# Skip weights carried by two existing loads, 14 instead of 17 zero matmuls, and a new order of work on every engine

## The reference

```
q   = layernorm(x)                               # over the last axis, 256
kv  = einsum('bhil,bhjl->bijhl', k, k)           # k = v = ctx, all pairs of the 8 channels
y   = irfft(rfft(kv, 512) * rfft(ssm_kernel, 512))[..., :256]
out = y + kv * D                                 # D: one skip weight per head
x1  = x + einsum('bijhl,bhil->bjhl', out, q)
g   = silu(layernorm(x1) @ Wg'); u = layernorm(x1) @ Wu'
out = x1 + (g * u) @ Wd'                         # W' = (int - 128) * scale
```

## Time and profile before

| | us |
|---|---|
| median of 3 runs | 78.2 (78.01 to 78.25) |
| profiled execution, first to last instruction (span) | 76.7 |
| PE busy | 70.7 (92%) |
| DVE busy | 63.9 (83%) |
| POOL busy | 54.6 (71%) |
| ACT busy | 46.7 (61%) |
| memory traffic | 8.29 MB, nearly all before 25 us |

### The profile page before, as it was taken

How to read it: one execution, slowest core, us unless ns; L and a number is a source line. 1 busy time by engine, 2 the same in 40 slices (tenths; PEclk the granted TensorE clock), 3 DMA queues, 4 the chain that set the end, 5 groups by cost and what they waited for, 6 DMA issues and landing times.

```text
span 76.7 us, 1495 instructions
## 1 busy us (share of the span) xinstructions
PE 70.7 (92%) x469; PEld 57.8 (75%) x469; DVE 63.9 (83%) x191; ACT 46.7 (61%) x115; POOL 54.6 (71%) x73
## 2 busy tenths in 40 slices
PE   4999988879999999999999999999999999999920
PEld 3767735568798777787888797988897989899810
DVE  0088399969999999899999999999999993786760
ACT  0601483275859587976868468746767798766400
POOL 5004798799889599299899949459627899939230
PEclk9999999999999999999999999999999999999995
DMA  0498999999997000000000000000000222200404
GB/s 5 132 256 279 386 344 295 285 384 397 386 353 220 13 0 0 0 0 4 4 9 0 0 0 0 0 0 0 0 9 4 68 68 68 68 9 0 137 0 137
DMA packets 7304, 8.29 MB, mean 108 GB/s; under 512 B 992, under 2 KB 6400, under 8 KB 7296
## 3 DMA queue, kind: packets, MB, share of 16 engines
q1 hardware_dynamic: 6912, 8.00, 31.7%
q10 hardware_dynamic: 384, 0.19, 0.8%
HBM read 7.12 MB, written 1.07 MB: 107 GB/s over the span
## 4 chain that ended last, share of the span: by engine, by line
PE 58%; DMA 15%; DVE 14%; SPq 3%; ACT 3%; issue 2%; DVEq 0%; ACTq 0%
PE conv L1010 18%; PE turn L957 8%; PE down L1029 8%; DMA k_ext<-ctx_ext 8%; DMA toeplitz<-taps 7%; PE conv L977 6%; PE conv L988 6%; PE conv L986 6%; DVE hidden L733 3%; DVE terms L718 2%; PE turn L939 2%; DVE terms L721 2%; PE turn L1029 2%; SPq L310 2%; ACT gate_act L508 1%
## 5 line engine op out<-in xcount | busy, mean ns | idle before, releaser
L1010 PE MATMUL conv<-f_parts,wgu 128*128 128x256 f16 x176 | 21.6, 273 | 0.3
L1010 PEld LDWEIGHTS conv<-f_parts,wgu 128*128 128x128 f16 x176 | 16.7, 98 | 3.5 <-DVE hidden L733 0.8
L376 POOL TENSOR_TENSOR products<-k_ext 128x512 f32<-128x512 f32 (+1 forms) x16 | 18.0, 1144 | 0.6 <-DMA k_ext<-ctx_ext 0.6
L508 ACT ACTIVATE gate_act<-conv,sg_sb 128x256 f32<-128x256 f32 (+1 forms) x24 | 11.2, 471 | 4.6 <-PE conv L1010 4.0
L258 POOL TENSOR_TENSOR h_lo<-hidden,h_hi 128x256 fp32r<-128x256 f32 x18 | 12.9, 729 | 1.4 <-ACT h_hi L513 1.3
L733 DVE SCALAR_TENSOR_TENSOR hidden<-conv,su_sb,gate_act 128x256 f32<-128x256 f32 (+1 forms) x24 | 11.3, 479 | 3.1 <-ACT gate_act L508 2.7
L977 PE MATMUL conv<-products,toeplitz 128*128 128x288 f32 x32 | 11.2, 434 | 0.3 <-DVE terms L725 0.3
L365 POOL TENSOR_TENSOR rstd_f<-variance_f,minus_half 128x1 f32<-128x1 f32 x8 | 5.5, 683 | 7.9 <-DVE variance_f L694 7.9
L718 DVE TENSOR_TENSOR terms<-conv,q_ext 128x512 f32<-128x512 f32 x16 | 10.8, 678 | 0.0
L986 PE MATMUL conv<-products,toeplitz 128*128 128x288 f32 x32 | 10.8, 422 | 0.0
L988 PE MATMUL conv<-products,toeplitz 128*128 128x288 f32 x32 | 10.4, 406 | 0.0
(11 more groups left out here) (64 smaller groups left out, 119.8 us busy)
## 6 DMA issues: line engine op xcount, KB each, us to landing
k_ext<-ctx_ext SPq DMA_DIRECT2D x3, 384.0 KB, 6.1
toeplitz<-taps_pad SPq DMA_DIRECT2D x2, 512.0 KB, 7.9
out<-x_sb SPq DMA_DIRECT2D x8, 128.0 KB, 1.7
toeplitz<-taps SPq DMA_DIRECT2D x3, 256.0 KB, 5.3
wg_int<-wg_t SPq DMA_DIRECT2D x1, 704.0 KB, 8.2
wu_int<-wu_t SPq DMA_DIRECT2D x1, 704.0 KB, 9.5
wd_int<-wd_t SPq DMA_DIRECT2D x1, 640.0 KB, 8.6
x_sb<-x SPq DMA_DIRECT2D x1, 512.0 KB, 7.0
```

What stands on the lines that cost most here:

```text
L376: nc.gpsimd.tensor_tensor(view(products[:, n:n + 1], first * MADE + GROUP, [[MADE, halves], [GROUP, 4], [1, GROUP]]), view(k, 0, [[EXT * B ...
L508: nc.scalar.activation(gate_act[up_lanes(t), i % 2, t, :], gate_of(i, t), ACT.Silu, scale=sg_sb[gate_lanes(t), t:t + 1]).then_inc(gate_act ...
L1010: done = nc.tensor.matmul(bank_of(i, t)[:, n, :], wgu[:, c, column:column + P], f_parts[:, i % 2, part, c, :], start=(c == 0 and part == 0 ...
```

## The change

1. `skip_all` is no longer a load of its own. The 16 weights stand ahead of each partition's row of k in memory, and the first k transfer brings them along (208 instead of 192 numbers a partition).
2. `skip_sb` is gone too. The weights stand in column 0 of the taps array, which was padding, and POOL reads them from there. POOL now waits for one transfer and not for two.
3. DVE no longer waits for `skip_loaded`.
4. `fill` issues 14 zero matmuls and not 17.
5. The lists of calls of PE, DVE, ACT and POOL are written in a new order. What they contain is otherwise the same; SP's list is the same.

```diff
-        skip_sb = sb("skip_sb", [H, 1])
-        skip_all = sb("skip_all", [P, H])
+        k_skip = sb("k_skip", [P, H + H * HALVES * EXT * B])
+        skip_all = k_skip[:, 0:H]
+        k_ext = k_skip[:, H:].rearrange("p (h c n) -> p h c n", h=H, c=HALVES)
...
             def load_k(first, last, done):
-                sp.dma_start(k_ext[:, first:last], ctx_ext[:, first:last]).then_inc(done, 16)
+                row = HALVES * EXT * B
+                columns = slice(H + first * row if first else 0, H + last * row)
+                sp.dma_start(k_skip[:, columns], ctx_skip[:, columns]).then_inc(done, 16)
...
-                nc.gpsimd.tensor_tensor(taps_sb[:, P:P + 1], taps_sb[:, P:P + 1], skip_sb[:, :],
+                nc.gpsimd.tensor_tensor(taps_sb[:, P:P + 1], taps_sb[:, P:P + 1], taps_sb[:, 0:1],
...
-            pool.wait_ge(taps_loaded, 32)
+            pool.wait_ge(taps_loaded, 16)
...
-            act.dma_start(skip_all[:, :], skip.rearrange("h a -> (h a)").partition_broadcast(P)).then_inc(skip_loaded, 16)
             act.dma_start(x_sb[:, 0, :], x[0:P, :]).then_inc(x_loaded[0], 16)
             act.dma_start(taps_sb[:, :], taps).then_inc(taps_loaded, 16)
-            act.dma_start(skip_sb[:, :], skip).then_inc(taps_loaded, 16)
...
             all_products(0, 0, 1)
+            dve.wait_ge(x_loaded[0], 16)
+            stats_of_q(0)
             all_products(0, 1, 2)
             dve.wait_ge(anti_ready, 1)
-            dve.wait_ge(skip_loaded, 16)
...
-            fill(turn[:, 0:2 * P], 17)
+            fill(turn[:, 0:2 * P], 14)
```

More of the change, by code:

```diff
@@ L71, in up_lanes, with build @@
     return slice(0, P) if t < FULL else slice(TAIL, P)
-def build(nc, x, ctx_ext, taps, skip, wg_t, s_gate, wu_t, s_up, wd_t, s_down, taps_pad, out):
+def build(nc, x, ctx_skip, taps, wg_t, s_gate, wu_t, s_up, wd_t, s_down, taps_pad, out):
     with ExitStack() as ctx:
@@ L578, in _ @@
             gate(0, 0)
-            wrap(4)
             gate(0, 1)
             hidden_high(0, 0)
-            squares(15)
+            wrap(4)
+            norm_q(6)
             gate(0, 2)
-            norm_q(6)
+            act.wait_ge(k_loaded[5], 16)
+            squares(12)
+            evict_q(5)
+            evict_q(6)
             hidden_high(0, 1)
-            evict_q(5)
+            gate(0, 3)
             hidden_high(0, 2)
-            gate(0, 3)
+            gate(0, 4)
+            hidden_high(0, 3)
+            squares(13)
             norm_f(2)
-            evict_q(6)
-            hidden_high(0, 3)
-            gate(0, 4)
+            wrap(5)
+            norm_f(3)
+            high_f(2)
+            gate(0, 5)
+            squares(14)
             norm_q(7)
[L594 to L597, removed]
             high_f(3)
+            evict_q(7)
             hidden_high(0, 4)
-            evict_q(7)
-            wrap(6)
             hidden_high(0, 5)
             gate(1, 0)
+            norm_f(4)
+            squares(15)
             gate(1, 1)
-            hidden_high(1, 0)
-            norm_f(4)
-            hidden_high(1, 1)
+            wrap(6)
             gate(1, 2)
             high_f(4)
+            hidden_high(1, 0)
             gate(1, 3)
+            gate(1, 4)
+            hidden_high(1, 1)
             hidden_high(1, 2)
@@ L613, in _ @@
             norm_f(5)
-            gate(1, 4)
             high_f(5)
@@ L777, in _ @@
             stats_of_q(2)
+            stats_of_q(3)
             moments_of_q(2)
-            shift_of_q(1)
             multiply_terms(0)
-            stats_of_q(3)
-            variance_of_q(2)
             multiply_terms(1)
             moments_of_q(3)
+            variance_of_q(2)
+            multiply_terms(2)
+            variance_of_q(3)
             dve.wait_ge(direct_loaded[3], 16)
@@ L1089, in _ @@
             convolve(11)
+            turn_q(6, x1_ready, 4)
             gates(0, 3)
             gates(0, 4)
-            turn_q(6, x1_ready, 4)
+            sum_terms(4, q_ready, 7)
             convolve(12)
-            sum_terms(4, q_ready, 7)
+            downs(0, 0)
             gates(0, 5)
-            downs(0, 0)
             turn_f(2, x1_ready, 5)
@@ L1102, in _ @@
             gates(1, 0)
+            downs(0, 1)
+            sum_terms(5, q_ready, 8)
             gates(1, 1)
-            downs(0, 1)
+            gates(1, 2)
+            turn_f(4, x1_ready, 6)
             downs(0, 2)
-            sum_terms(5, q_ready, 8)
-            gates(1, 2)
             downs(0, 3)
-            turn_f(4, x1_ready, 6)
-            gates(1, 3)
             downs(0, 4)
             downs(0, 5)
+            gates(1, 3)
+            gates(1, 4)
             sum_terms(6, f_ready, 5)
             convolve(15)
-            gates(1, 4)
             gates(1, 5)
@@ L1137, in _ @@
             gates(3, 2)
+            downs(2, 3)
             gates(3, 3)
-            downs(2, 2)
-            downs(2, 3)
             downs(2, 4)
```

234 lines of the change are left out of this document (114 added, 120 removed).

## The result

The changed kernel takes 84.5 us (84.2 to 84.7, 4 runs) against 78.2 (78.0 to 78.3, 4 runs): 8.2% slower, ratio 1.082, 95% interval 1.079 to 1.085. Forecast were 77.2 us, with a range of 76.2 to 78.3 and a chance of 0.14 for slower. The profiled execution was timed at 84.48 us, its span is 82.6. Times are medians of all runs of a kernel; a few runs were in a slower state, and the ratios leave those out.

The account below looks back on a forecast made before the run. PE and DVE, both full from 20.1 to 30.6 us, were taken as the bound, with time winnable before. Span 76.7 + 0 (loads) + 0 (fill) - 1.0 (early order) + 0 (later) = 75.7, plus 1.5 gives 77.2 us; range 76.2 to 78.3.

Parts of the forecast that it names:

- the sum over DVE: DVE up to 25 us: same work, transfer waits 1.65 us where 2.49 were; with small stops, a lead of 1.0 us.
- a new order takes no work from it: Argument against a later gain on DVE, full from 43.8 to 55.5 us; that rival: 76.4 us, chance 0.18.
- the bound of +1.0 for the later lists: From 25 us to the end: new order counted 0, bounds -1.2 and +1.0, for PE holes closed or opened.
- The lead before 25 us: Start to head 8: PE ahead by 1.2 us, DVE by 1.0; the smaller, 1.0, was taken off the span.
- DVE's 2.49 us of waits for transfers: DVE's waits at 4.87, 8.90 and 16.28 us (0.32, 1.42, 0.75) in the old trace, forecast to become 1.65.
- PE's 0.68 at 15.76: PE's wait for a normalized q tile before the turn of tile 2, forecast to go as its norm comes earlier.
- the new wait in front of the first turn: After head 0 ends at 7.40 us, PE waits 0.6 us for tile 0's norm, until 8.02.
- the 1.5 us between span and median: Last step of the sum: median taken as 1.5 us above the span, turning 75.7 into 77.2 us.
- the 832 B for a piece of 768 B of k1: k transfers: rows start 64 B off, so each 768 B piece fetches 832 B, 8% more; no change to the sum.
- The clock rival: PE's rise from half pace, 6.9 us before, comes later; with 6 us delay, 79.1 us; chance 0.10.
- the loads at 0: Start of kernel: dropping two small loads and enlarging k0 counted 0, bounds -0.3 and +0.3 us.
- the three zero matmuls at 0: PE's fill: three fewer zero matmuls gain nothing, as PE then stands until toeplitz0 at 4.87 us.

Follow-up runs that it names:

- the replacement: `direct` and DVE's merges replaced by a one-SBUF-input `bn_stats`: on the changed kernel 78.23 us, ratio 1.0006; on the kernel before 77.80 us, 0.997.
- only `direct` replaced: Changed kernel with only its 8 `direct` instructions replaced by a `bn_stats` with one SBUF input: 80.81 us, ratio 1.040.
- The two early moves: Kernel before, new loads, `variance_of_q(1)` ahead of `direct(2)`, `norm_q(2)` and `wrap(0)` ahead of `squares(8)`: 78.25 us; without the `variance_of_q(1)` move 78.27 us.

## Why the prediction was wrong

**The step that failed is the sum over DVE: "Its work is the same; only waits can go", and with it "a new order takes no work from it".** An instruction's length was taken as its own, from whatever row showed it. For DVE's instructions with two SBUF inputs the length depends on what POOL is doing at that moment. The order of before has them in POOL's gaps, beside its short roots, or a little ahead of its long instructions: in its trace all eleven merges on DVE lie between 0.67 and 0.69 us. The new order puts `direct(6)`, `direct(7)` and most merges (eight of eleven above 0.7 us) behind the start of one of POOL's instructions. The prediction's walk through the lists put "0.6 us of `direct` and one more `multiply_terms`" ahead of 17.2 us without a look at POOL, which the trace of before has busy there with products:

```profile
14.52 6.21 POOL L376 TENSOR_TENSOR products<-k_ext 128x512 f32<-128x512 f32 x5
```

Measured: 5.9 us, what the replacement gives in the changed kernel (6.3) less what it gives in the kernel before (0.4). No rival had this mechanism, and the range's end of 78.3 and the bound of +1.0 for the later lists had no term for it.

**The lead before 25 us was not there either.** With the conflict gone from both kernels, head 8 starts like this, first in the new order and then in the old:

```profile
25.15 0.65 PE L975 MATMUL conv<-products,toeplitz 128*128 128x288 f32 x2
```

```profile
24.75 0.65 PE L977 MATMUL conv<-products,toeplitz 128*128 128x288 f32 x2
```

The new order is 0.4 us behind here. Another trace of it, with only `direct` replaced and the same lists up to 25 us, has 24.59, so such a start moves by half a microsecond from one execution to the next, and the two orders are level at 25 us, where the forecast had PE 1.2 and DVE 1.0 ahead. The times differ by 0.4 (78.23 and 77.80), and what the later lists give back lies within that. Two terms of the lead were wrong.

The first is what there was to win. DVE's 2.49 us of waits for transfers and PE's 0.68 at 15.76 came from a single execution. With the same DVE list up to there, DVE waits 1.71 us in the trace of the 14 zero matmuls, 1.76 in those of the loads alone and of the replacement, and 2.02 in that of `direct(7)` moved; the 0.75 for x is 0 to 0.28 in these, and PE's 0.68 is 0 to 0.19. So most of the 0.8 us between 2.49 and the 1.65 forecast was no property of the order. The 1.65 itself came out at 1.64 by luck: x0 and toeplitz2-3 cost nothing (0.4 and 0.85 forecast), toeplitz0 0.31, and x1 1.33 where 0.4 was forecast.

The second is the new wait in front of the first turn: 0.6 us forecast, 0.8 by pitch in the changed kernel (7.85 to 8.69, with head 0 itself later) and 2.9 in the one without conflict. DVE waits there for x of tile 1, and the shift of tile 0 stands behind the stats of tile 1:

```profile
7.57 0.43 DVE L662 BATCH_NORM_STATS2 stats_q<-x_sb 128x6 f32<-128x256 f32 x1 [1.50 <-DMA x_sb<-x]
8.03 0.18 DVE L666 BATCH_NORM_AGGREGATE moments_q<-stats_q 128x2 f32<-128x6 f32 x1
8.13 0.18 DVE L675 TENSOR_SCALAR shift_q<-moments_q,rstd_q 128x1 f32<-128x1 f32 x1
```

In the trace of before DVE came to that x late, so its landing was only bounded, and the walk used it as if it were known: the shift was taken to come in time for a turn at 8.02, and came at 7.73 and here at 8.13.

Two smaller slips: the 1.5 us between span and median joined two different executions. Every run that has both shows 1.7 to 1.9, so the profiled execution of before was some 0.3 us slower than the median, an estimate. And the 832 B for a piece of 768 B of k1 hold only for some rows: a partition's row is now 12352 B, 64 more than a multiple of 256, so rows stand 0, 64, 128 or 192 B off in turn. It was no term of the sum.

**The clock rival had the right picture and the wrong cause.** The late doubling is there (13.7 us), as "what would show it" described it. But the time didn't hang on it: 84.06, 84.49 and 84.53 us go with a pace that doubled at 6.1 (and fell back), 9.7 and 13.7. Its price of half the delay was too high here; that DVE sets the pace is the likely reason (DVE is 59% of the chain that ended last in the changed kernel, 14% in the kernel before), but it was argued and not tested.

**Right were** the loads at 0 (0.9995), the three zero matmuls at 0 (1.003), the later lists within 0.4 us of the 0 they were given, the conflict apart, and that toeplitz0 sets head 0, at 4.84. The wait for x at 16.28 and the one before the turn of tile 2 went, but they are gone or small in other traces of the old lists too, so they are no sign for the mechanism. The two early moves are worth nothing in time.

## What to carry to other kernels

Before a new order is costed, lay DVE's instructions with two SBUF inputs beside POOL's long ones; a meeting cost DVE up to 1.0 us here (0.34 became 1.36 beside POOL's 1.26), and the trace shows it as a longer instruction and not as a wait. A comparison of mean ns by line and form between two traces of the same work shows it. If DVE's own instructions show no stretch, compare POOL's: before this change it was POOL that waited (1.78 us for 1.28), and a new order can turn that round. And a wait that is to be won back should stand in more than one trace of the old kernel.

## What was not expected of the hardware

- Two DVE instructions of 0.34 us in a row took 2.63 us beside POOL's products of 1.26: POOL starts its next instruction before the second gets its turn, so each waits out about one whole POOL instruction.
- It works both ways: POOL's `low` beside a DVE merge showed 1.17 us instead of 0.73.
- A DVE instruction that reads one input from PSUM (0.68 us, 16 of them in each kernel) or only one from SBUF (bn_stats, 0.68 for 512 elements) isn't touched.
- The moment at which PE's pace doubles moved between executions from 4.5 us or earlier to 13.7 us, and from 5.1 to 13.7 between two kernels whose lists are alike up to 18 us; where it could be compared it cost some 0.5 us or less.
